# A recurrence with top-2 expert routing on one core: the recurrent stage's side work is placed anew, and the centring of the second weights moves from VectorE to ScalarE

## What is computed

```python
def layer(x, adj):                               # x, adj: 128 x 128 x 128, float32
    s = layernorm(x)
    beta = (s @ e_weight) / max(sum(adj, axis=2), 1e-7)
    agg = einsum('blu,blm->bmu', beta, adj)
    h = 0                                        # batch x 128
    for t in range(128):                         # the recurrence, one step for each position
        h = tanh(agg[:, t] @ Wx + h @ Wh + b); y[:, t] = h
    x1 = x + y
    z = layernorm(x1)                            # 16384 tokens of 128
    logits = z @ gate_w + gate_b                 # 16 experts, the best two, softmax of the two
    moe = sum over the two of w * (relu(z @ w1[e] + b1[e]) @ w2[e] + b2[e])
    return x1 + layernorm(z + moe) * gamma + beta
```

## Time and profile before

| | us |
|---|---|
| median of 3 runs | 909.22 |
| lowest and highest | 905.97, 914.53 |
| span of the profiled execution | 901.8 |
| aggregation | 0 to 76 |
| recurrent stage, first to last tanh | 76 to 292 |
| tables | 292 to 326 |
| first pass | 326 to 588 |
| second pass | 588 to 902 |

### The profile page before, as it was taken

The page is one execution under the profiler, slowest core; times in us unless marked ns, Lnnn a source line. Parts: engine busy times, 40 slices in busy tenths (PEclk is TensorE's granted clock), DMA queues, the critical chain, the costliest instruction groups (busy, mean ns, idle before and its releaser), DMA issues.

```text
span 901.8 us, 18429 instructions
## 1 busy us (share of the span) xinstructions
PE 614.3 (68%) x4132; PEld 544.6 (60%) x4133; DVE 576.9 (64%) x2941; ACT 377.7 (42%) x1186; POOL 502.0 (56%) x553
## 2 busy tenths in 40 slices
PE   3668777887787247777887688556666677776670
PEld 3555555666666247766776577556655676666560
DVE  6995877767787846766676666625555556555462
ACT  3995332222222034433444344254455464554440
POOL 4666676666676716655555556605445546444455
PEclk9999978768777569989889989877788888877886
DMA  9996676787586534454444444163443434344320
GB/s 229 292 295 153 157 232 198 247 286 242 185 258 234 88 84 154 162 157 151 142 143 144 147 138 135 43 215 103 135 140 112 133 113 154 109 131 135 104 69 11
DMA packets 127503, 143.39 MB, mean 159 GB/s; under 512 B 17115, under 2 KB 112073, under 8 KB 127440
## 3 DMA queue, kind: packets, MB, share of 16 engines
q1 hardware_dynamic: 108368, 99.18, 38.3%
q0 software_dynamic: 17920, 42.97, 13.6%
q10 hardware_dynamic: 1152, 0.55, 0.4%
HBM read 68.60 MB, written 78.30 MB: 163 GB/s over the span
## 4 chain that ended last, share of the span: by engine, by line
PE 33%; another core or an unknown queue 10%; ACT 9%; issue 6%; POOL 2%; ACTq 2%; DVE 1%; DMA 1%; SPq 0%; POOLq 0%; DVEq 0%
PE bank L924 17%; PE bank L940 13%; ACT hs L994 4%; ACT xT L975 3%; PE bank L913 2%; ACT wr L983 2%; PE bank L937 2%; POOL out_dram L205 1%; ACTq L193 1%; POOL rows_by_second L205 1%; DVE R L1051 1%; DMA R<-rows_by_second 0%; ACTq L983 0%; DMA rows_by_second<-R 0%
## 5 line engine op out<-in xcount | busy, mean ns | idle before, releaser
L924 PE MATMUL bank<-xT,wr 128*128 128x128 f32 x1152 | 186.5, 314 | 131.7 <-ACT xT L975 118.4
L924 PEld LDWEIGHTS bank<-xT,wr 128*128 128x128 f32 x1152 | 167.4, 224 | 143.3 <-issue 115.9
L994 ACT ACTIVATE hs<-bank,wr 128x128 f32<-128x128 f32 x432 | 127.2, 369 | 263.7 <-remote 132.8
L205 POOL DMA_INDIRECT out_dram<-R x144 | 141.2, 981 | 164.4 <-DVE R L1105 126.4
L205 POOL DMA_INDIRECT rows_by_second<-R x144 | 145.9, 1013 | 124.0 <-DVE R L1073 79.9
L1073 DVE SCALAR_TENSOR_TENSOR R<-bank,R 128x128 f32<-128x128 f32 x288 | 87.3, 345 | 170.5 <-PE bank L940 86.2
L940 PE MATMUL bank<-W,hs 128*128 x1152 | 195.7, 310 | 0.0
L940 PEld LDWEIGHTS bank<-W,hs 128*128 128x128 f32 x1152 | 168.3, 210 | 6.2
L205 POOL DMA_INDIRECT rows_by_first<-st,idx x128 | 130.0, 1016 | 54.9 <-issue 36.2
L983 ACT COPY wr<-W1b 128x258 f32 x288 | 104.9, 426 | 30.7 <-PEq L789 19.7
L517 ACT ACTIVATE HT<-bank,bcol 128x128 f32<-128x128 f32 x128 | 46.9, 366 | 147.0 <-PE bank L436 88.9
(11 more groups left out here) (141 smaller groups left out, 942.4 us busy)
## 6 DMA issues: line engine op xcount, KB each, us to landing
rows_by_second<-filler SPq DMA_DIRECT2D x6, 4704.0 KB
R<-rows_by_second SPq DMA_DIRECT2D x36, 784.0 KB
R<-rows_by_first SPq DMA_DIRECT2D x144, 67.5 KB
xq<-in_x_dram SPq DMA_DIRECT2D x32, 256.0 KB, 4.1
aq<-in_adj_dram SPq DMA_DIRECT2D x32, 256.0 KB, 4.7
x2r<-in_x_dram SPq DMA_DIRECT2D x32, 256.0 KB
rows_by_second<-R POOLq DMA_INDIRECT x144
out_dram<-R POOLq DMA_INDIRECT x144
```

What stands on the lines that cost most here:

```text
L205: return nc.gpsimd.indirect_dma_start(dst, bass.IndirectOffsetOnAxis(ap=idx, axis=0), src, None, bounds_check=limit[n], oob_is_err=False)
L924: i = mm(ps_h[c][h][:, (j % 2) * P:(j % 2 + 1) * P], wr[:, u % 2, j, c * P:(c + 1) * P], xT[:, u % 2, j * P:(j + 1) * P], start=True, stop ...
L994: i = a(hs[:, h, c, k * P:(k + 1) * P], ps_h[c][h][:, k * P:(k + 1) * P], ACT.Relu, bias=wr[:, u % 2, 2 * h + k, F + c:F + c + 1])
```

## The change

- `fresh` makes one product with 128 columns instead of a quarter of one with 512; all four write one bank, one is issued behind each of the four steps instead of all behind step 0.
- On TensorE `turn_h` moves from behind step 1 to behind step 0, and `count` from behind step 2 to behind step 1. `logits` stays behind step 2 and `turn_x` behind step 3.
- The three centring operations leave VectorE's list. ScalarE gets two: `w2_mean` behind tanh 2 (Identity with scale -1/128, its sum accumulated into a column of `w2m`) and `w2_centre` behind tanh 3 (Identity with that column as bias, in place).
- GpSimd's `send` gets a part: two scatters of a quad in one turn, two in the next, ahead of that turn's root.

```diff
@@ -86,7 +86,8 @@
         b2lo = sb("b2lo", [P, P], BF16)
         b2s = sb("b2s", [P, P], BF16)
         b2m = sb("b2m", [P, 1])
-        w2m = sb("w2m", [P, 1])
+        w2m = sb("w2m", [P, 2 * NE])
+        w2junk = sb("w2junk", [P, P])
         sel = sb("sel", [P, NE, P], BF16)
         gm_bc = sb("gm_bc", [P, P])
         bt_bc = sb("bt_bc", [P, P])
@@ -312,10 +313,11 @@
                 pool.wait_ge(s_v2, q + 1)
                 g.tensor_tensor(st[:, u, :, C_RSTD], ve2[:, h, :], mhalf[:, 0:QUAD], ALU.pow).then_inc(s_r2, 1)
 
-            def send(q, u):
-
-                hold(pool, s_d, q + 1)
-                for j in range(QUAD):
+            def send(q, u, part):
+
+                if part == 0:
+                    hold(pool, s_d, q + 1)
+                for j in range(2 * part, 2 * part + 2):
                     scatter(dram_a.ap(), idx1[:, u, j:j + 1], st[:, u, j, :], ROWS_A).then_inc(s_sct[u], 16)
 
             quads(pool, scale, SLOTS)
@@ -351,14 +353,18 @@
             rest()
 
             def turn(q, u):
+                if beyond(q, 4):
+                    send(q - 4, (u - 4) % SLOTS, 1)
                 if beyond(q, 1):
                     rstd(q - 1, (u - 1) % SLOTS)
                 if beyond(q, 3):
-                    send(q - 3, (u - 3) % SLOTS)
+                    send(q - 3, (u - 3) % SLOTS, 0)
             quads(pool, turn, SLOTS)
+            send(NQ - 4, SLOTS - 4, 1)
             rstd(NQ - 1, SLOTS - 1)
             for k in range(3):
-                send(NQ - 3 + k, SLOTS - 3 + k)
+                for part in range(2):
+                    send(NQ - 3 + k, SLOTS - 3 + k, part)
 
 
         @block.tensor
@@ -422,9 +428,10 @@
                            skip_group_check=True)
                 i.then_inc(s_cnt, 1)
 
-            def fresh(q, u):
-
-                return mm(ps_rnn[u % 2][:, :], Ec[:, :], AX[:, bass.ds(QUAD * q, QUAD), :], start=True, stop=True,
+            def fresh(q, u, k):
+
+                return mm(ps_rnn[u % 2][:, k * P:(k + 1) * P], Ec[:, :],
+                          AX[:, bass.ds(QUAD * q + k, 1), :].rearrange("p o b -> p (o b)"), start=k == 0, stop=True,
                           skip_group_check=True)
 
             def steps(q, u):
@@ -436,11 +443,11 @@
                         mm(ps_rnn[u % 2][:, k * P:(k + 1) * P], Wh_sb[:, :],
                            HT[:, h, ((k - 1) % QUAD) * P:((k - 1) % QUAD + 1) * P], start=False, stop=True,
                            skip_group_check=True).then_inc(s_rn, 1)
-                    if k == 0 and not (isinstance(q, int) and q == NQ - 1):
-                        fresh(q + 1, u + 1)
-                    if k == 1 and beyond(q, 1):
+                    if not (isinstance(q, int) and q == NQ - 1):
+                        fresh(q + 1, u + 1, k)
+                    if k == 0 and beyond(q, 1):
                         turn_h(q - 1, u - 1)
-                    if k == 2 and beyond(q, 3):
+                    if k == 1 and beyond(q, 3):
                         count(q - 3, u - 3)
                     if k == 2 and beyond(q, 2):
                         logits(q - 2, u - 2)
@@ -449,7 +456,9 @@
 
             quads(pe, agg, SLOTS)
             pe.wait_ge(s_ae, NQ)
-            fresh(0, 0).then_inc(s_rn, 1)
+            for k in range(QUAD):
+                i = fresh(0, 0, k)
+            i.then_inc(s_rn, 1)
             for u in range(SLOTS):
                 steps(u, u)
             with pe.Fori(1, NQ // SLOTS - 1) as J:
@@ -520,6 +529,25 @@
                         x1T_out(q - 2, u - 2)
                     if k == 1 and beyond(q, 3):
                         exps(q - 3, u - 3)
+                    if k == 2:
+                        w2_mean(q)
+                    if k == 3:
+                        w2_centre(q)
+
+            w2v = W2[:, :, :, :].rearrange("p e c f -> p (e c) f")
+
+            def w2_mean(q):
+                if isinstance(q, int) and q == 0:
+                    act.wait_ge(r_b2, 16 * 4)
+                else:
+                    hold(act, w2_ok, 2 * q)
+                a(w2junk[:, :], w2v[:, bass.ds(q, 1), :].rearrange("p o f -> p (o f)"), ACT.Identity, scale=-1.0 / P,
+                  accum_out=w2m[:, bass.ds(q, 1)]).then_inc(w2_ok, 1)
+
+            def w2_centre(q):
+                hold(act, w2_ok, 2 * q + 1)
+                w = w2v[:, bass.ds(q, 1), :].rearrange("p o f -> p (o f)")
+                a(w, w, ACT.Identity, bias=w2m[:, bass.ds(q, 1)]).then_inc(w2_ok, 1)
 
             quads(act, first, SLOTS)
             agg_out(NQ - 1, UN - 1)
@@ -720,28 +748,12 @@
 
 
 
-            w2v = W2[:, :, :, :].rearrange("p e c f -> p (e c) f")
-
-            def centre_1(q, u):
-                if beyond(q, 1):
-                    dve.wait_ge(w2_ok, 3 * q)
-                v.tensor_reduce(w2m[:, :], w2v[:, bass.ds(q, 1), :], AX_X, ALU.add).then_inc(w2_ok, 1)
-
-            def centre_2(q, u):
-                dve.wait_ge(w2_ok, 3 * q + 1)
-                v.tensor_scalar(w2m[:, :], w2m[:, :], -1.0 / P, None, ALU.mult).then_inc(w2_ok, 1)
-
-            def centre_3(q, u):
-                dve.wait_ge(w2_ok, 3 * q + 2)
-                w = w2v[:, bass.ds(q, 1), :].rearrange("p o f -> p (o f)")
-                v.tensor_scalar(w, w, w2m[:, :], None, ALU.add).then_inc(w2_ok, 1)
-
             def turn(q, u):
 
 
                 order = ((tile_a, 1), (soft_1, 3), (tile_b, 1), (soft_2, 3), (place_1, 3), (tile_b2, 1), (place_2, 3),
                          (soft_3, 3), (tile_b3, 1), (gate_1, 2), (place_3, 3), (gate_2, 2), (place_4, 3), (gate_3, 2),
-                         (centre_1, 0), (gate_4, 2), (centre_2, 0), (gate_5, 2), (centre_3, 0))
+                         (gate_4, 2), (gate_5, 2))
                 for part, lag in order:
                     if beyond(q, lag) and not (isinstance(q, int) and q - lag >= NQ):
                         part(q - lag, (u - lag) % SLOTS)
@@ -899,7 +911,7 @@
                 mm = nc.tensor.matmul
                 pe.wait_ge(r_w, 16 * 5)
                 pe.wait_ge(r_pool, 9)
-                pe.wait_ge(w2_ok, 3 * NQ)
+                pe.wait_ge(w2_ok, 2 * NQ)
                 pe.wait_ge(tables, 1)
 
                 def turn(r, G, u):
```

## The result

The kernel before was run again beside the changed one. Medians of 12 runs each: 912.25 us before (905.97 to 918.12), 912.62 us after (909.10 to 914.67). The comparison gives a ratio of 1.0053, its 95% interval 1.0032 to 1.0075, which would be a cost of about 4.8 us (912 x 0.0053; 2.9 to 6.8). It is not the quotient of the medians listed, which lie only 0.4 us apart (1.0004), and how it weighs the single runs is not known. A second comparison in another group of runs gave 1.0044 (1.0008 to 1.0079), with medians of 910.96 and 913.66 us. So the change costs something between nearly nothing and 0.7%; by either reading the gain of 4.6 us that I forecast (904.6 us) is not there, and by both ratios the sign is the other way. The profiled execution after took 912.56 us.

What follows compares the result with a forecast made beforehand. It saw GpSimd's scatters at 6.13 us a quad, plus waits including late releases closing a 7.3 us ring, as the bound; -1 - 2 - 1.6 = -4.6 on 909.2 (901.8 span, median 7.4 over) gave 904.6 us, range 886 to 918.

Steps and rivals of the forecast that it cites:

- fresh in four: TensorE, recurrent stage: eight 128-column instructions replace two of 512; taken as 0, bounds -1 to +4 us.
- The base: Whole kernel: profiled span 901.8 us, median of the runs 7.4 over it, carried over as 909.2.
- The quad of 7.36 us at the half level: Recurrent stage: a quad bound by TensorE at its half clock takes 7.36 us between last tanhs and stays.
- the ring: Recurrent stage, late quads: four scatters 4.9, release 0.8, VectorE to place_4 1.6, together 7.3 us against GpSimd's 6.13.
- rival 3: TensorE waits at count and gets the half clock in more quads: +7 us, 916, up to 925; chance 0.17.
- the 27.4: GpSimd's waits in the recurrent stage: 27.4 us, all it can give back while the scatters stay as they are.
- Split send: GpSimd's scatters divided over two turns: same instruction order, only the loop's back edge moves; -3 to +3, taken as 0.
- First scatter: Pipeline fill of the recurrent stage: earlier turn_h brings the first scatter up to a step earlier, -1 us.
- Two late quads of VectorE's own: Recurrent stage: two quads where VectorE was late though the logits were there gain -1 us each.
- the loop edges: VectorE's three loop edges that made GpSimd wait 1.8 us: moving the centring gains -0.5 each, -1.6 us.
- Centring on ScalarE: Two Identity operations behind tanh 2 and tanh 3, 0.39 us each, fit in a step: cost 0, bound +4.
- count's wait: TensorE waits for VectorE's hot one step sooner, holding step 2 and logits: cost 0, bound +9 us.

Runs made afterwards that it cites:

- h1: Kernel before with only the input part in four products, in a group where the kernel before took 925.7 us: 931.44 us, ratio 1.0064.
- e4: Kernel before with only the input part in four products, in a group where the kernel before took 719.4 us: ratio 0.9994.
- g4: Kernel before with only the input part in four products, in a group where the kernel before took 718.9 us: ratio 0.9981.
- n1: Changed kernel with GpSimd's root between the second and third scatter, against the kernel before at 925.8 us: 918.86 us, ratio 0.9903.
- f1: Changed kernel run again unaltered, against the kernel before at 911.0 us: 913.66 us, ratio 1.0044.
- e3: Changed kernel with the second weights centred on VectorE again, in three instructions per quad, against the kernel before at 719.4 us: ratio 1.0001.
- k1: Changed kernel with one input product, logits behind step 1, count behind step 2, place_3 and place_4 before gate_1; kernel before 910.4 us: 911.63 us, ratio 0.9985.
- e1: Changed kernel with logits moved behind step 1 and count behind step 2 on TensorE, against the kernel before at 719.4 us: ratio 0.9991.
- g2: Changed kernel with place_3 and place_4 ahead of gate_1 on VectorE, against the kernel before at 718.9 us: ratio 0.9984.
- m2: Kernel before with logits behind step 1 and GpSimd's root between the second and third scatter, against the kernel before: ratio 1.0040.

## Why the prediction was wrong, point by point

In short: the term for `fresh` in four stood at 0 and measured +5.9 us. With it the sum would give +1.3 us instead of -4.6. The rest of the miss is gains that were counted and did not come, since what was saved on VectorE turned into waiting for the logits.

**The base.** The sum was made against 901.8 us and the median was taken to stand 7.4 over the span for some reason outside it. The execution after shows 912.56 against a span of 910.8: only 1.8 us lie around a span. The execution profiled before was an unusually short one: its time was near 903.6, where the 12 runs of that kernel have their least at 905.97 (another held group has one at 901.15 beside a median of 911.0). Part of that lies outside the recurrent stage: it has the shortest part behind the scatters of all held traces, 584.5 us. That the ring closes more often in its median execution may be, but is not shown: the changed kernel's two traces both have 25 such steps. The gain of 4.6 was computed on single late quads of that execution, below what differs between executions.

**fresh in four: the term that was mis-sized.** In the prediction's sum it stood at 0, with bounds of -1 and +4 us "in quads at the half level". h1 measures +0.64% of 925.7 = 5.9 us (3.6 to 8.2, so the upper bound was just inside what is measured) for this edit alone, in a held group; in two free groups it cost nothing (e4, g4). The reference I used was the aggregation's group of eight instructions, 1.26 us a quad, in a stage in which TensorE has the full clock nearly throughout; here the four products come to 59.8/31 = 1.93 us a quad against 43.7/31 = 1.41. So TensorE's part grew by 0.5 us in a quad that I knew to be bound by TensorE's completions. Through what instruction this becomes time stays open. The Trainium skill ("TensorE: Matmul & The Clock Gate", section on LDWEIGHTS), by whose price of a load the prediction put 20 us as the far end, has the right sign in the held group and three times the size, and neither in the free ones.

**The quad of 7.36 us at the half level: misread.** In its window, 198.40 to 205.76, the granted clock is 0.69 on average, between the levels, and the tanhs at both its ends waited 3.24 and 2.33 us. It is one turn of the ring, 7.36 as above, and not the pace of TensorE's own work; so the limit for `fresh` and the threshold of rival 3 rested on the wrong cause. The list of GpSimd's waits, too, names 22.2 us of the 27.4 (16.9 for place_4, 5.3 for the variance).

**Split send, 0: right.** GpSimd's stream is the old one, root and then four scatters (143.04 to 147.93 above). The change's third part, as a root between the scatters, doesn't take place; n1, where it does, is 1.4% faster held.

**First scatter, -1: right.** 93.52 against 94.98 before, and 93.96 in f1. It brings nothing, since the ring behind it takes no notice of an earlier start.

**Two late quads of VectorE's own, -2, and the loop edges, -1.6: wrong by their place.** VectorE is lighter (148.3 us busy against 162.6) and its issue gaps in front of tile_a fell from 16.8 to 6.4 us. But the way to the next scatter then leads through gate_1, which stands for the logits until 0.8 us behind the scatters: its wait grew from 15.5 to 52 us. This is read from the traces; no held run has these edits alone.

**Centring on ScalarE, 0: not contradicted.** e3 shows no difference free. Held, all parts but the four products together are worth 1.0044 to 1.0053 over 1.0064, -0.1 to -0.2%, inside both intervals. No separate held run was made of it.

**Ring and rivals.** The working of the ring (4.9 + 0.8 + 1.6 = 7.3) is confirmed: 7.36 measured, in 25 of 31 steps. I had it in hand and then used it only as a fixed background, "a ring that the scatters close anyway". It closed in two thirds of the quads, and an edit could close it in the rest; by my estimate from the two traces (19 and 25 steps, 7.36 - 6.13 = 1.2 us each) six more steps are 7 us. The rival that went slower had the right sign and about the right size (+7 us) and the wrong mechanism: neither count's wait (3.5 us) nor the clock (0.80). The 27.4 us that I gave as all that can be won from GpSimd's waits are real: free groups have them all, 196.2 us from first scatter to last.

## What to carry to other kernels

When a late event closes a ring, ask of each edit not only what it costs but whether it closes the ring in quads that are still open; price it at the difference between the two periods. Keep an instruction that releases another engine (place_4) out of the queue behind one that waits for a late event (gate_1); and expect that a ring opened at one wait closes at the next completion, so that two gains of 1% may add to none, as in k1. Judge a single profiled execution against the spread of the times before summing microseconds on it.

## What the runs showed of the hardware that I had not expected

The same kernel took 719 us in four groups and 910 to 926 us in four others, both on one and the same chip, with scatters of the same 970 ns and ScalarE operations of the same 127 us in all. Of the busy time only TensorE's differs much (617.7 us against 549.4 for products and 573.0 against 512.4 for loads, changed kernel against e1, at a granted clock of 0.82 against 0.90); the rest of the difference is idle time. In the held groups a tanh starts up to some 3 us behind the issue of its product while GpSimd scatters (4.4 in n1), and then mostly 0.7 to 1.1 us behind the end of a scatter (27 of the 29 that are over 1 us late in the changed kernel, 17 of 23 before); in the free groups it doesn't. The Trainium skill ("SBUF — State Buffer", Practical consequences) says, of contention for SBUF's ports, that PE and ACT never wait on anyone. In the free groups nothing speaks against it; in the held ones ScalarE's tanh waits up to 3.37 us for TensorE (above), and no run here shows whether a port has to do with it. What decides between the two kinds, I could not find; nothing that a kernel of mine changed did.

The differences between orders also exist only held: the edits here were worth -1.2% to +0.6% there, and in free groups at most 0.2% either way (g4 -0.2%, g2 -0.2%, the divided root +0.1%), but for m2's +0.4%.
